# Four slots for gathered expert rows, gathers six tiles ahead, and all four quarters of the next activations split before the expert tiles

## The reference, cut to what matters

```python
x = x + xattn(layernorm(x), ctx)          # x: 8 x 224 x 2048, ctx: 8 x 750 x 2048, softmax attention
h = layernorm(x)
base_out   = h @ base_w.T + base_b        # 2048 -> 2048
res_hidden = h @ A.T                      # 2048 -> R = 64
probs      = softmax(h @ router_w.T)      # E = 16 experts
topw, topi = top_k(probs, 2);  topw = topw / (sum(topw) + 1e-6)
delta = sum over e of combine[e] * (res_hidden @ B[e].T)     # B: 16 x 2048 x 64
x = x + base_out + delta * 0.5
```

## Time and profile before

| what | value |
|---|---|
| median of 3 runs | 1538.42 us (1529.47 to 1540.98) |
| the profiled execution, its own time | 1535.22 us |
| its span (first to last instruction) | 1533.5 us |
| mean granted TensorE clock | 0.957 |
| PE busy | 1386.5 us, 90% |
| DVE, ACT, POOL busy | 62%, 41%, 21% |
| DMA queue of SP's transfers, of POOL's | 61.0%, 11.4% of 16 engines' span |

### The profile page before, as it was taken

How to read it: one execution, slowest core, us unless ns; L and a number is a source line. 1 busy time by engine, 2 the same in 40 slices (tenths; PEclk the granted TensorE clock), 3 DMA queues, 4 the chain that set the end, 5 groups by cost and what they waited for, 6 DMA issues and landing times.

```text
span 1533.5 us, 18405 instructions
## 1 busy us (share of the span) xinstructions
PE 1386.5 (90%) x6777; PEld 1121.6 (73%) x6777; DVE 948.0 (62%) x1199; ACT 630.4 (41%) x797; POOL 319.4 (21%) x247
## 2 busy tenths in 40 slices
PE   5889999999999999998997779877788999999998
PEld 4668787777878787876886657755566778888886
DVE  5467777677776867774572646554557664555543
ACT  3354554545455555453210546554556621011100
POOL 1001102020202020103217323334344111111110
PEclk9989999999999999998999889888898999999999
DMA  6967778686878686695645698797886788888884
GB/s 226 272 195 248 218 245 259 206 257 209 251 236 263 218 266 215 209 218 171 196 137 159 191 300 228 201 297 209 246 260 169 250 290 262 240 240 244 259 256 130
DMA packets 216840, 350.59 MB, mean 229 GB/s; under 512 B 26992, under 2 KB 129392, under 8 KB 207088
## 3 DMA queue, kind: packets, MB, share of 16 engines
q1 hardware_dynamic: 198192, 282.31, 61.0%
q0 software_dynamic: 10528, 52.85, 11.4%
q10 hardware_dynamic: 8064, 14.68, 2.8%
HBM read 266.11 MB, written 99.41 MB: 238 GB/s over the span
## 4 chain that ended last, share of the span: by engine, by line
PE 32%; DMA 12%; DVE 4%; ACT 3%; issue 2%; POOL 2%; SPq 1%; ACTq 0%; POOLq 0%; DVEq 0%
PE scores L821 10%; PE scores L822 9%; PE scores L823 9%; DMA b_in<-in_bT_dram,brow_i 6%; DMA res<-x_scratch 4%; ACT b_hl L1029 2%; POOL hs_scratch L1566 1%; PE work L857 1%; DMA w_in<-in_wT_dram 1%; PE work L858 1%; DVE b_hl L1410 1%; DVE a_l L1368 1%; SPq L561 1%; DVE w_l L1361 1%; DMA a_in<-xT_scratch 1%
## 5 line engine op out<-in xcount | busy, mean ns | idle before, releaser
L821 PE MATMUL scores<-w_h,a_h 128*128 128x512 f32 x896 | 359.0, 401 | 60.8 <-DVE a_l L1368 56.6
L822 PE MATMUL scores<-w_l,a_h 128*128 128x512 f32 x896 | 355.1, 396 | 0.0
L823 PE MATMUL scores<-w_h,a_l 128*128 128x512 f32 x896 | 354.8, 396 | 0.0
L821 PEld LDWEIGHTS scores<-w_h,a_h 128*128 128x128 f32 x896 | 171.8, 192 | 103.8 <-DVE a_l L1368 51.3
L1014 ACT ACTIVATE a_h<-a_in 128x512 fp32r<-128x512 f32 x168 | 93.9, 620 | 314.6 <-DMA a_in<-xT_scratch 204.6
L1368 DVE TENSOR_TENSOR a_l<-a_in,a_h 128x512 fp32r<-128x512 f32 x168 | 130.4, 824 | 124.8 <-ACT a_h L1014 120.6
L823 PEld LDWEIGHTS scores<-w_h,a_l 128*128 128x128 f32 x896 | 171.2, 191 | 38.9
L822 PEld LDWEIGHTS scores<-w_l,a_h 128*128 128x128 f32 x896 | 171.8, 192 | 37.6
L691 PE MATMUL scores<-ctxT_h,nT_h 128*112 128x494 f32 (+1 forms) x512 | 175.0, 342 | 10.1 <-DVE ctxT_l L1119 6.7
L1129 DVE TENSOR_TENSOR raw_l<-raw_in,val_h 128x512 fp32r<-128x512 f32 x192 | 154.9, 826 | 45.5 <-ACT val_h L945 45.3
L790 PE MATMUL scores<-val_h,eT_h 128*112 128x512 f32 (+1 forms) x384 | 159.5, 415 | 19.2 <-DVE raw_l L1129 17.5
(11 more groups left out here) (153 smaller groups left out, 1903.6 us busy)
## 6 DMA issues: line engine op xcount, KB each, us to landing
ctxT_in<-in_ctxT_dram SPq DMA_DIRECT2D x64, 750.0 KB, 6.6
a_in<-xT_scratch SPq DMA_DIRECT2D x42, 1024.0 KB, 9.4
raw_in<-in_ctx_dram SPq DMA_DIRECT2D x32, 1280.0 KB
w_in<-in_wT_dram SPq DMA_DIRECT2D x32, 512.0 KB, 11.1
x<-in_x_dram SPq DMA_DIRECT2D x8, 1792.0 KB, 10.6
xT_scratch<-xT_st SPq DMA_DIRECT2D x8, 1792.0 KB, 11.8
res<-x_scratch SPq DMA_DIRECT2D x56, 256.0 KB, 7.9
y_add<-y_scratch SPq DMA_DIRECT2D x56, 256.0 KB, 5.5
```

What stands on the lines that cost most here:

```text
L821: pe.matmul(o, ah, wh, start=(k == 0), stop=False)
L822: pe.matmul(o, ah, wl, start=False, stop=False)
L823: last = pe.matmul(o, al, wh, start=False, stop=(k == KD - 1))
```

## The change

1. `b_in` gets four slots in the place of two, in the same bytes per partition: tiles with s % 4 below 2 go to partitions 0 to 63, the others to 64 to 127 (`halves`). A tile in the upper half has its high part in the upper half of `b_hl` and its low part in the lower one.
2. Four gathers are issued at once when the routing is done, two more in turn 11, and after the scatter of s the gather of s+6, which waits for the low part of s+2.
3. `ROUTING` is now every turn 0 to 27: all four quarters of the next activations are split ahead of the expert tiles.
4. The scatters of the hidden values start one turn earlier (`SCATTER_AT` 6 to 9), the first expert work one turn later (`Y_FIRST_AT` 11), there with the two expert splits ahead of the entries' split. `Y_TILES` is now two tiles in turns 12 and 13 and three in each of 14 to 26; no turn is without them and none has four.

```diff
+    BR = 4
-        b_in = over(at_nT, "b_in", [R, 2, D])
+        b_in = over(at_nT, "b_in", [P, 2, D])
+        def halves(s):
+            same, other = slice(0, R), slice(R, P)
+            return (same, other) if s % BR < 2 else (other, same)
-        HR_AT, ROUTE_AT, COUNT_AT, PLACE_AT, SCATTER_AT = 3, 4, 6, 6, (7, 8, 9, 10)
-        Y_FIRST_AT = 10
-        ROUTING = (ROUTE_AT, ROUTE_AT + 1, PLACE_AT)
+        HR_AT, ROUTE_AT, COUNT_AT, PLACE_AT, SCATTER_AT = 3, 4, 6, 6, (6, 7, 8, 9)
+        Y_FIRST_AT = 11
+        ROUTING = tuple(range(PAIRED))
-        for g in (11, 12) + tuple(range(TT + 1, 2 * TT - 1)):
-            count = min(4 if g == TT + 1 else 3, SL - n)
+        for g in range(TT - 2, 2 * TT - 1):
+            count = min(2 if g < TT else 3, SL - n)
-        Y_BEHIND = {3: (3, 8, 13), 4: (2, 6, 10, 14)}
+        Y_BEHIND = {2: (4, 11), 3: (3, 8, 13)}
             def expert_high(s):
-                act.activation(b_hl[0:R, s % 2, :], b_in[:, s % 2, :], ACT.Copy).then_inc(b_high, 1)
+                same, other = halves(s)
+                act.activation(b_hl[same, s % 2, :], b_in[same, s % 2, :], ACT.Copy).then_inc(b_high, 1)
             def expert_low(s):
-                dve.tensor_tensor(b_hl[R:P, s % 2, :], b_in[:, s % 2, :], as_f32(b_hl[0:R, s % 2, :]),
+                same, other = halves(s)
+                dve.tensor_tensor(b_hl[other, s % 2, :], b_in[same, s % 2, :], as_f32(b_hl[same, s % 2, :]),
             def load_expert(s):
-                if s >= 2:
-                    pool.wait_ge(b_ready, s - 1)
+                if s >= BR:
+                    pool.wait_ge(b_ready, s - BR + 1)
-                        load_expert(0)
-                        load_expert(1)
+                        for s in range(BR):
+                            load_expert(s)
                 if g == Y_FIRST_AT:
-                    load_expert(2)
-                    load_expert(3)
+                    load_expert(BR)
+                    load_expert(BR + 1)
                 for s in Y_TILES.get(g, []):
                     scatter_out(s)
-                    if s + 4 < SL:
-                        load_expert(s + 4)
+                    if s + BR + 2 < SL:
+                        load_expert(s + BR + 2)
```

More of the change, by code:

```diff
@@ L387, in xattn_ffn_kernel @@
         yrow_ready = sem("yrow_ready")
-        b_loaded = [sem(f"b_loaded{i}") for i in range(2)]
+        b_loaded = [sem(f"b_loaded{i}") for i in range(BR)]
         b_high = sem("b_high")
@@ L1026, in expert_high @@
             def expert_high(s):
-                act.wait_ge(b_loaded[s % 2], (s // 2 + 1) * 16)
+                act.wait_ge(b_loaded[s % BR], (s // BR + 1) * 16)
                 at_least(act, y_done, (s - 1) * NC)
-                act.activation(b_hl[0:R, s % 2, :], b_in[:, s % 2, :], ACT.Copy).then_inc(b_high, 1)
+                same, other = halves(s)
+                act.activation(b_hl[same, s % 2, :], b_in[same, s % 2, :], ACT.Copy).then_inc(b_high, 1)
             def rows_out(s):
@@ L1091, in _ @@
                 if g == Y_FIRST_AT:
-                    slots_high(0)
                     expert_high(0)
                     expert_high(1)
+                    slots_high(0)
                 for s in Y_TILES.get(g, []):
@@ L1485, in _ @@
                 if g == Y_FIRST_AT:
-                    slots_low(0)
                     expert_low(0)
                     expert_low(1)
+                    slots_low(0)
                 for s in Y_TILES.get(g, []):
@@ L1569, in load_expert @@
             def load_expert(s):
-                if s >= 2:
-                    pool.wait_ge(b_ready, s - 1)
+                if s >= BR:
+                    pool.wait_ge(b_ready, s - BR + 1)
                 else:
                     pool.wait_ge(route, PLACED)
-                pool.indirect_dma_start(b_in[:, s % 2, :], None, bT.rearrange("e r d -> (e r) d"),
+                same, other = halves(s)
+                pool.indirect_dma_start(b_in[same, s % 2, :], None, bT.rearrange("e r d -> (e r) d"),
                                         bass.IndirectOffsetOnAxis(ap=brow_i[:, s:s + 1], axis=0)
-                                        ).then_inc(b_loaded[s % 2], 16)
+                                        ).then_inc(b_loaded[s % BR], 16)
             def scatter_out(s):
```

## The result

| | before | after |
|---|---|---|
| median of the runs | 1534.84 us (1529.47 to 1540.98, 4 runs) | **1471.06 us** (1468.69 to 1477.88, 4 runs) |
| ratio, with its 95% interval | | 0.959 [0.955, 0.964] |
| the profiled execution, its own time | 1535.22 us | 1477.88 us |
| its span | 1533.5 us | 1476.1 us |
| mean granted TensorE clock | 0.957 | 0.973 |

Predicted were 1456 us and a range of 1430 to 1495: the range holds the result, the number is 15 us too low, and the forecast's own band, 1441 to 1470, is missed by 1 us. (With the 3.2 that the prediction adds for the median they make 1456.9, not 1456.) The median run took 6.8 us less than this one, and in which turns no profile tells.

A forecast was written before the change was run, and what follows sets the result against it. The bound was taken as latency: a gather issued some 16 us into a turn is wanted at its end. Turns 10 to 26 summed to 300.4 against 381.9 us, gaining 81.5: 1453.7, plus 3.2 for the median, given as 1456; range 1430 to 1495.

The forecast's parts named there:

- the forecast's own band: Whole kernel: 1441 to 1470 us, from turns 15 to 26 at 17.2 to 19.5 us each; chance 48%.
- the ring: Kernel before, turns 15 to 26 at 23.3 us: residual landing, bias addition, gather issue and landing, split, in a chain.
- Quarters at nothing: Steady turns: splitting all quarters first ends the 41.8 us of waits for `a_l`, but by itself only moves the wait.
- The upper half of the slots at nothing: Upper half of `b_in` and `b_hl`: splits cost 0 extra, between -0.3 and +0.3 us a tile.
- The 27 us: Turn 14, change of chunk with three expert tiles: 16.5 + 10.5 = 27 us, bounds 20 and 32.
- if SP is held again at turn 13: A sign that the forecast is wrong; before, SP was held 11.17 us in the issue of `res`.
- What is late next: Turns 15 to 26: three `y_out` slots, POOL's queue and `res` make two turns take about 34.5 us, 17.2 each.
- without the pairs of long and short: Sign expected in the profile after: turns 15 to 26 at 17 to 19.5 us, no long turn alternating with a short.
- 1 to 3 us each: Sign expected after: ACT's and DVE's rows out wait this long for `y_scratch`, as the new last wait.
- the DMA engines are full: Rival, 22%: gathers delay other transfers, two turns take 34.5 + 6 us, 19.5 to 22 a turn; 1470 to 1500 us.
- the first rival: Rival, 22%: the loop falls under PE's own time, turns 15 to 26 at 16.7 us; 1430 to 1441 us.
- PE alone: Rival, 22%: PE's own work alone bounds turns 15 to 26, 16.7 us each; 1430 to 1441 us.

The follow-up runs named there:

- Quarters only: The kernel before with one edit, all four quarters of the next activations split first in every turn; 1537.85 us, ratio 1.0025.
- lead four: The changed kernel with its four slots, but gathers four tiles ahead instead of six and none in turn 11; 1520.72 us, ratio 0.9896.
- bias last on the kernel before: The kernel before with POOL's bias addition put behind the scatters and gathers of the turn; 1493.77 us, ratio 0.9722.
- bias last: The changed kernel with POOL's bias addition for turn g+2 behind the scatters and gathers in turns with expert tiles; 1466.27 us, ratio 0.9546.
- wide gathers and the bias last: The changed kernel with gathers as 4 KB rows into all 128 partitions and POOL's bias addition behind scatters and gathers; 1434.7 us, ratio 0.935.

## Why the prediction was right, and where it fell short

- **The bound before** was named rightly: a latency behind POOL's residual wait, with `a_l` only its last link. Quarters only (no gain, the wait moved to the rows out), lead four (the gain gone) and bias last on the kernel before (41 us by taking one link out of the ring) show it from three sides.
- **Quarters at nothing**: right, twice.
- **The upper half of the slots at nothing**: right. The splits take 1.912 us on ACT and 2.286 on DVE in the median of both halves, as in the earlier trace rows.
- **The start**, turns 10 to 13: 53.8 us forecast, 52.1 measured. The entries' load, put between 841 and 848, and PE's wait for it, put at 2 us, by the timeline (start, duration, what, idle time before):

```profile
844.93 1.00 SPq L609 DMA_DIRECT2D hs<-hs_scratch  x2
...
847.28 0.36 PEld L843 LDWEIGHTS scores<-ident,hs 128*64 128x64 f32 x4 [0.44 <-DMA hs<-hs_scratch]
```

- **Turn 14: the first step that failed**, 12.0 us of the 21.5. The 27 us came from DVE's order of work alone, with weights landing as in the earlier trace rows. They landed in up to 24.61 us, while 11.7 MB moved from 865 to 904 us (300 GB/s at a share of 1.05). That could have been read beforehand: between 892 and 914 us the kernel before was at a share of 1.02 and 305 GB/s, and the change lays the gathers and scatters of two tiles in turn 13 and three in turn 14 about that place. A sum of bytes was made for turns 15 to 26 and not for this turn. The prediction's own list has a sign close to it, "if SP is held again at turn 13": the issue of turn 13 took 4.45 us, that at the start of turn 14 was held for 22.18. And PE's long wait, 12.18 us, was not for `w_l` or the fourth bank but for ACT's copy: the forecast had followed DVE's order of work, and the late weights told on ACT's.
- **Turns 15 to 26: the mechanism held, the size did not**, 11.2 us. "What is late next" named the `y_out` slots, POOL's queue and `res` as the new loop, and rows of after show just that. It put the loop at 34.5 to 36.5 us for two turns; turns 18 to 25 take 40.4. The term that was mis-sized is the landing of `res`: 13.5, at most 15.5 taken, measured 20 to 21 for the rows that SP asks for at the start of turns 17, 19, 21 and 23; in three of the four, 13 of them are SP's issue. In the turns between, 16, 18, 20 and 22, they landed in 6.3 to 8.5, and the median of the twelve is 11.2, lower than before: a median doesn't tell what the link of a loop takes. So "without the pairs of long and short" was wrong from turn 18 on, and "1 to 3 us each" was 3.1 in the mean of ACT's 16 waits, but up to 7.0. The list's sign "if a turn is still above 21" came true in turns 18, 20, 22 and 24 (23.2 to 24.0). Its "290 to 330 GB/s" did not, with 271; the forecast's own bytes, 62.5 MB in 12 x 18.3 us, give 285.
- **The rival "the DMA engines are full"** had the truer cause. Its loop of 34.5 + 6 is what turns 18 to 25 show (40.4), in part by luck: it put 3 us each on the landings of `res` and `y_scratch`, where in the chain `res` grew by 7 and the scatters landed in 5 to 6 us, sooner than the 8.5 taken. Turns 15 to 17 and 26 ran near PE's pace, so the time landed at its lowest end and at the edge of the forecast. Its mark is that bias last took the loop away and the time stayed. The forecast's 17.9 us of DMA time a turn was good (18.2 measured); what was missed is that a resource at 17.9 of 18.3 us leaves no room for transfers to land at the times of a kernel with a share of 0.77.
- **A rule and its row.** The busy DMA engines moved 271 / 0.95 = 285 GB/s, as the row of before gave it (290), and not the 425 GB/s that the prediction quoted from the Trainium skill; by its 12.3 us a turn the first rival would have come in. Even with wide gathers and the bias last it is 306 / 0.88 = 348.
- **PE alone** (22%) was wrong for this kernel, but is what it does once the DMA time is less: 16.8 us a turn in wide and bias last, as that rival had it.

## What to carry to other kernels

When a change takes away a latency, add up the bytes of every stretch it touches, the odd turns too, against the rate at which the engines move them when busy; if that comes near the time forecast, landing times read from the slack kernel need not hold any more. Before adding buffers, look at what stands in a queue ahead of the transfer that is late, and at the shape of its destination: here an addition moved behind it and rows spread over all partitions, with no new slot, brought more (77 us) than slots, lead, order and the earlier start together (64). When a wait is relieved and only another one grows, ask which resource both share.

## What the runs showed of the hardware

- **A gather into 64 partitions costs DMA time.** With the same bytes into 128 partitions in rows of half the length, POOL's queue moved 391 GB/s in place of 313, the gathers' own packets took 328 ns per 8 KB in place of 606, and all DMA time of the twelve turns fell from 219 to 178 us. The Trainium skill ("SBUF — State Buffer", "Door 1: The DMA port swizzle (why `[64,N]` ≈ `[32,N]`)") says that a DMA's rate depends on how many of the 16 ports its partitions reach, and that partitions 0 to 63 and 64 to 127 lie on different halves of them; the trace agrees in direction, in the rates just given. Destination and row length were changed together here; the scatters' 309 ns for 8 KB speak against the length, but no run tells the two apart.
- **Transfers that nobody edited got cheaper with it**: SP's queue went from 76 to 61 us for the same 17.42 MB. So the time that the profile gives a queue holds what others do to it.
- **An issue can hold its queue for long**: SP stood 22.18 us in the issue of 256 KB of residual rows in turn 14, and 13 us at the start of turns 17, 19 and 21, against 1.9 to 5.5 in the others of 15 to 26, so that all behind it started late.
